# Moving three transposes in a step-scheduled attention and Mamba kernel: the second residual from step 30 to 19, x1 from step 2 to 3

## What is computed

```
q, k, v = wq x + bq, wk x + bk, wv x + bv        # 32, 32 and 256 channels, 4096 positions
x1  = gamma * (v softmax(q^T k)^T) + x            # layer 0: attention over all 4096 positions, and the residual
u   = layernorm over channels(x1) * norm_g + norm_b
z, xBC, dt = in_w u                               # 256, 512 and 4 channels
xBC = silu(causal depthwise conv of 4 taps(xBC) + conv_b)
y   = state space scan over the positions (4 heads of 64, 128 states, decay exp(dt * A)) + Dp * xs
out = out_w (rmsnorm(y * silu(z)) * rms_w)
x   = x1 + out * sigmoid(se2(relu(se1(mean of out over the positions)) ))   # gate per batch and channel
```

## Time and profile before

| | |
|---|---|
| three runs, median | 3153.75 us (3151.14 to 3154.02) |
| the profiled execution | 3150.87 us, its span 3148.7 us |
| TensorE (PE) busy | 2980.0 us, 95% |
| VectorE (DVE) busy | 2032.0 us, 65% |
| ScalarE (ACT) busy | 1930.0 us, 61% |
| GpSimd (POOL) busy | 2009.9 us, 64% |
| mean granted TensorE clock | 0.983 of full speed |

### The profile page before, as it was taken

The page is one execution under the profiler, slowest core; times in us unless marked ns, Lnnn a source line. Parts: engine busy times, 40 slices in busy tenths (PEclk is TensorE's granted clock), DMA queues, the critical chain, the costliest instruction groups (busy, mean ns, idle before and its releaser), DMA issues. The chain is left out here.

```text
span 3148.7 us, 63156 instructions
## 1 busy us (share of the span) xinstructions
PE 2980.0 (95%) x21208; PEld 2322.5 (74%) x21208; DVE 2032.0 (65%) x3417; ACT 1930.0 (61%) x3742; POOL 2009.9 (64%) x3087
## 2 busy tenths in 40 slices
PE   6899999999999999999999999999999999999984
PEld 3767777777777777777777777777777777777762
DVE  5556666666666676676676666676666667666654
ACT  2565666666656566666665666666666666666652
POOL 2446666667756576666676656666676667777753
PEclk9999999999999999999999999999999999999986
DMA  3111111111311121222221222122221111212121
GB/s 123 49 37 46 44 51 58 31 54 49 103 63 65 58 71 58 91 77 74 82 77 38 72 76 72 62 76 69 65 89 36 43 49 55 69 50 69 42 95 67
DMA packets 101970, 200.99 MB, mean 64 GB/s; under 512 B 18480, under 2 KB 41392, under 8 KB 97264
## 3 DMA queue, kind: packets, MB, share of 16 engines
q1 hardware_dynamic: 98192, 195.08, 18.6%
q10 hardware_dynamic: 3456, 1.86, 0.2%
HBM read 131.21 MB, written 64.75 MB: 62 GB/s over the span
## 5 line engine op out<-in xcount | busy, mean ns | idle before, releaser
L723 POOL TENSOR_TENSOR p_lo<-p,p_hi 128x512 f16<-128x512 f32 x1024 | 1221.9, 1201 | 845.6 <-ACT p_hi L886 711.9
L879 ACT ACTIVATE p<-p_et 128x512 f32<-128x512 f32 x1024 | 612.2, 598 | 637.4 <-PE p_et L1138 598.0
L1156 PE MATMUL acc<-v_hi,p_hi 128*128 128x257 f16 x4096 | 954.3, 273 | 4.0 <-DVE work L1464 3.8
L1158 PE MATMUL acc<-v_lo,p_hi 128*128 128x256 f16 x4096 | 951.8, 272 | 0.0
L1420 DVE TENSOR_REDUCE maxes<-p_mx 128x1 f32<-128x1024 f32 x508 | 620.1, 1221 | 489.1 <-PE p_mx L1117 488.7
L886 ACT ACTIVATE p_hi<-p 128x512 f16<-128x512 f32 x1024 | 643.5, 629 | 10.0
L1164 PE MATMUL acc<-v_hi,p_lo 128*128 128x257 f16 x4096 | 622.8, 274 | 15.1 <-POOL p_lo L723 15.1
L1156 PEld LDWEIGHTS acc<-v_hi,p_hi 128*128 128x128 f16 x4096 | 399.3, 97 | 125.0 <-issue 54.8
L1158 PEld LDWEIGHTS acc<-v_lo,p_hi 128*128 128x128 f16 x4096 | 400.6, 98 | 117.8 <-issue 49.9
L1164 PEld LDWEIGHTS acc<-v_hi,p_lo 128*128 128x128 f16 x4096 | 399.9, 98 | 68.0 <-POOL p_lo L723 15.9
L1138 PE MATMUL p_et<-qs,kst 98*128 98x256 f16 x2048 | 393.3, 273 | 11.6 <-ACT p L879 11.1
(11 more groups left out here) (213 smaller groups left out, 4164.2 us busy)
## 6 DMA issues: line engine op xcount, KB each, us to landing
work<-rows_d SPq DMA_DIRECT2D x32, 1024.0 KB, 5.2
xin<-in_x_dram SPq DMA_DIRECT2D x48, 512.0 KB, 4.7
xr<-in_x_dram SPq DMA_DIRECT2D x32, 512.0 KB, 3.8
x_d<-x1c SPq DMA_DIRECT2D x31, 512.0 KB, 2.9
og_d<-og SPq DMA_DIRECT2D x29, 512.0 KB, 2.7
mix_x<-x_d SPq DMA_DIRECT2D x25, 512.0 KB, 4.7
mix_o<-og_d SPq DMA_DIRECT2D x24, 512.0 KB, 5.5
out_dram<-mix_o SPq DMA_DIRECT2D x24, 512.0 KB, 2.8
```

Source lines behind the costliest of these rows:

```text
L723: e.tensor_tensor(p_lo[:, n % RING, :], p32[:, n % P32S, :], p_hi[:, n % RING, :], ALU.subtract).then_inc(lo_pool, 1)
L879: e.activation(p32[:, n % P32S, :], p_et[:, :], ACT.Exp).then_inc(exp_done, 1)
L1156: e.matmul(acc[:, t, 0:C + 1], p_hi[:, r, at:at + P], v_hi[:, 2 * k + kk, 0:C + 1], start=(k == 0 and kk == 0), stop=False)
L1158: e.matmul(acc[:, t, 0:C], p_hi[:, r, at:at + P], v_lo[:, 2 * k + kk, :], start=False, stop=False, skip_group_check=True)
```

## The change

Two constants change, and with them the place of the fill on TensorE, of the copy that empties it on ScalarE, and of the transfer that follows it on SyncE's queue. No instruction is added or removed.

```diff
-K_X1T, K_UT, K_DT, K_DAT, K_CUM, K_YT, K_OUT = 2, 9, 10, 21, 23, 30, 0
+K_X1T, K_UT, K_DT, K_DAT, K_CUM, K_YT, K_OUT = 3, 9, 10, 21, 23, 30, 0
-K_XT = (13, 30)
+K_XT = (13, 19)
```

## The result

| | before | after |
|---|---|---|
| median of five runs | 3153.21 us (3148.49 to 3154.02) | 3136.39 us (3133.51 to 3140.16) |
| the profiled execution, its span | 3150.87, 3148.7 us | 3134.20, 3132.1 us |
| mean granted clock | 0.983 | 0.982 |

The ratio of the runs is 0.9952, with a 95% interval of 0.9938 to 0.9966: faster by 16.8 us by the medians, and by 16.67 us between the two profiled executions. The forecast was 3137.5, in a range of 3123 to 3147.

What follows compares the result with a forecast made beforehand. TensorE, busy 2980.0 of 3148.7 us, was taken as the bound, so gains must come from its waits. Gains of 14.5 and 1.7 summed to 16.2 us, giving 3137.5 us by the median, range 3123 to 3147.

Steps and rivals of the forecast that it cites:

- Part A: Second `xT` moved from step 30 to 19: net 0.56 us less in a regular block, 14.5 us in all.
- the five blocks with a `v`: Blocks 4, 9, 12, 17, 20 at step 30: `v` then waits as `xT` did, winning only 0.13 us each.
- rival 3: The gain of step 30 is given back at step 8 as well: about 3150 us, chance 0.08.
- Rival 5: ScalarE becomes the bound in steps 19 to 21, `xT`'s copy delaying the exponential: 3162 us, chance 0.04.
- Part B: `x1T` moved from step 2 to 3: 0.52 us of wait gone, mostly given back at step 8; 1.7 us gain.
- The shift of GpSimd by the scan: In 19 blocks VectorE's earlier scan holds an earlier Newton step: GpSimd 0.1 us later each, -1.9 us in all.
- Room of 0.1 us before `x1T1`: At step 3, `mt` would end 0.1 us before `x1T1` asks for it: cost nothing, or a few tenths.
- Blocks 10, 18, 26: Blocks with the gate at steps 4 and 7, half a us before GpSimd binds: 0.3 us gain each.
- 8 and 16: Blocks where `mr` behind `st1` waits for VectorE, whose train moves with TensorE: 0.3 us gain each.
- The tail: Blocks 32 on, where `cb0` comes before `x1T` but its waits are for GpSimd: no change.
- Rival 2: The `x1T` move counts too, GpSimd's train being less fixed than it looks: 3123.7 us, chance 0.12.
- Rival 4: Stalls of blocks 9 and 17 lengthen and the slow-clock stretch behind doubles, costing 8 us: 3145 us, chance 0.08.

Runs made afterwards that it cites:

- a_only: Kernel before with only the second `xT` moved from step 30 to 19, `x1T` left at step 2; 3138.1 us, ratio 0.9959.
- ab_sum7: Changed kernel with GpSimd's first output sum moved from step 6 to 7; 3136.64 us, ratio 0.9946 to the kernel before.
- ab_mix14: Changed kernel with VectorE's mix of the previous batch two steps later (T_MIX 12 to 14); 3131.57 us, again 3132.65 us.
- b_only: Kernel before with only `x1T` moved from step 2 to 3, second `xT` left at step 30; 3152.27 us, ratio 1.0003.
- ab_sum7_mix14: Changed kernel with GpSimd's first output sum at step 7 and VectorE's mix at T_MIX 14; 3144.57 us, ratio 0.9964.

## Why the prediction was right, and where it was not

**Part A, 14.5 forecast, 13.7 measured in the tabled steps and 14.5 with the step that the table leaves out.** The step lengths came out to the hundredth: 2.85 and 1.98, net -0.56; in the five blocks with a `v` -0.15 for -0.13. Blocks 2 to 30 make 24 x 0.56 + 5 x 0.15 = 14.2, and the tabled sum has 0.4 less, because only the +0.44 of step 19 of block 31 is inside it. Its step 30 gives 0.77 in the tail, net 0.33 where 0.4 was counted. With it, part A measures 14.5 us. The reasons held too: `a_only` shows no wait at step 8 that grew, so everything behind step 30 does follow TensorE, and rival 3 is out. Rival 5 is out by the row of ScalarE above: the exponential has the room that was worked out.

**Part B, 1.7 forecast; about 1.9 measured without blocks 9 and 17, by other terms.** The cause, that GpSimd's train takes the gain back at step 8, was right (`ab_sum7`). Three of its terms were off:
- *The shift of GpSimd by the scan* had the wrong sign. Steps 2 to 9 of an ordinary block give -0.18, where the forecast had +0.1: GpSimd is 0.18 earlier, not 0.1 later. VectorE's scan and GpSimd's Newton steps after the change, against the earlier trace rows:

```profile
1490.01 1.22 DVE L1561 TENSOR_TENSOR_SCAN lt<-work,ident 128x512 f32<-128x512 f32 x1
```

```profile
1490.19 1.03 POOL L765 TENSOR_SCALAR nw<-nw 128x4 f32<-128x4 f32 x1 [0.16 <-issue]
1491.36 0.20 POOL L767 TENSOR_TENSOR nw<-nw 128x4 f32<-128x4 f32 x1
```

  The scan did hold the Newton step until its own end (1491.23), as the Trainium skill's page "SBUF — State Buffer", section "Who interferes with whom", has it. But it caught L765, one step earlier than before, and not L763: one more step follows behind it, not two. The train loses 0.34 us there and wins the 0.52 by which the scan ends earlier. So an ordinary block gives back 0.34 at step 8 (idle 0.73 for 0.39) where the forecast had 0.6. In blocks 11, 19 and 27 the wait of `st1` is gone behind the new wait for `mt`, and in blocks 14, 22 and 30 it did not grow. Its total is therefore 15.1 and not 23.
- *Room of 0.1 us before `x1T1`* was read off one block and taken for all. It holds in block 15 and in 25 others. In blocks 2, 11, 19 and 27 VectorE's train is later, and the trace of before shows it. Block 11 before, the start of step 2 and `mt`:

```profile
1108.44 0.38 PE L1138 MATMUL p_et<-qs,kst 98*128 98x256 f16 x2
...
1111.70 0.68 DVE L1569 TENSOR_TENSOR mt<-pl,lt 128x512 f32<-128x512 f32 x1
```

  TensorE would ask 2.85 us into the step (2.19 + 0.22 + 0.44), and `mt` ends 3.94 into it, with no idle time before it that could be won: the same sum as for block 15 gives a wait of 1.09 us here and in blocks 2, 19 and 27 (1.10, 1.08 and 1.07). It came as 1.06 in 11, 19 and 27. A small operation of VectorE is held by GpSimd in these blocks. Block 11 after the change, VectorE and TensorE:

```profile
1105.09 1.04 DVE L1477 TENSOR_SCALAR nw<-nw 128x4 int32<-128x4 int32 x1
1106.04 1.21 DVE L1420 TENSOR_REDUCE maxes<-p_mx 128x1 f32<-128x1024 f32 x1
1107.17 0.67 DVE L1569 TENSOR_TENSOR mt<-pl,lt 128x512 f32<-128x512 f32 x1
```

```profile
1107.99 0.63 PE L1171 MATMUL pl<-ident,work 128*128 128x128 f32 x4 [1.06 <-DVE mt L1569]
```

  In block 15 the same L1477 takes 0.49 us. Block 11 has a mix on VectorE at step 0, and with the mix moved away (`ab_mix14`) L1477 is back to 0.50 and the wait is gone. Block 2 has no mix; what makes its VectorE late before the change was not tested. But why its wait is 1.94 and not 1.10 stands in the traces. L1477 and GpSimd's next `low` (L723), before and after:

```profile
254.96 0.17 DVE L1477 TENSOR_SCALAR nw<-nw 128x4 int32<-128x4 int32 x1
255.87 1.16 POOL L723 TENSOR_TENSOR p_lo<-p,p_hi 128x512 f16<-128x512 f32 x1 [1.02 <-ACT p_hi L886]
```

```profile
255.51 1.04 DVE L1477 TENSOR_SCALAR nw<-nw 128x4 int32<-128x4 int32 x1
255.37 1.16 POOL L723 TENSOR_TENSOR p_lo<-p,p_hi 128x512 f16<-128x512 f32 x1
```

  Before, ScalarE's copy of `x1T` stood ahead of `p_hi` in step 2, and GpSimd idled for 1.02 us beside L1477. The change takes that copy away; GpSimd's `low` comes at once, and L1477 lasts 0.87 us longer beside it. Behind this wait the granted clock fell:

```profile
259.00:262.00 3.00, 3.00 (x16) 2.11 (x15) 0.00 (x0) 1.12 (x2) 2.12 (x8) 0.50 0.51 172
```

  All eight traces of kernels with B have this stretch in block 2, none of the six without B has it. The four blocks cost 4.8 us, where the forecast had a gain of 0.5 (block 2) and a loss of 0.3 (the other three). This is the step of part B that failed: *"nothing, or a few tenths"* was 1.06 and 1.94 us of idle time.
- *Blocks 10, 18, 26* gave 0.51 each where 0.3 was taken, and *8 and 16* 0.43 and 0.07 for 0.3 each. Blocks 4, 12 and 20 gave the 0.52 of the forecast.

That the errors of B cancel is luck: its 16 ordinary blocks gave 4.7 us more than forecast, and blocks 2, 11, 19 and 27 gave 5.0 less. That the median agrees with the forecast to 1.1 us is partly luck too: blocks 9 and 17 (+1.5), the rest of the attention and the start (+0.9) and the tail without part A's share (-2.5) were not in the sum, and they too nearly cancel.

**The tail, forecast at nothing.** Of its 3.3 us 0.8 are part A's step 30 of block 31. The other 2.5 are within what the same program shows from one execution to the next, so these traces show nothing against the forecast of no change, and they could not show a change of 1 or 2 us.

**Rival 2** (B counts in full) is out by `b_only`. **Rival 4** (the clock): the stalls of blocks 9 and 17 did grow, from 8.2 us of idle time in sum in both traces of before to 9.5 and 10.1 in the first two of the changed kernel. But both blocks together are 212.6, 211.3 and 211.4 us in three traces against 211.4 and 212.3 before, so the slow stretch did not double. What did come is a new slow stretch in block 2, where the forecast had no stall.

## What to carry to other kernels

When a bank is asked for in the same step in which its neighbour was filled, a move by a single step takes the wait away; look at the order of the fills before looking for a quiet place. A wait taken out of a bound engine counts as far as nothing behind it hangs on a train of another engine that started earlier: find the next wait behind the change and what anchors the engine it names. And the room read in one block is the room of that block: a new wait has to be priced in every kind of block, above all where another engine has a piece of work that comes only sometimes. Here the trace of before already had the four exceptions, at 1.1 us each.

## What the runs showed of the hardware

- A VectorE operation on 128x4 elements (L1477) took 0.17 us while GpSimd was idle (block 2 before) and 0.50 or 1.04 us beside GpSimd's elementwise operations (blocks 15 and 11), and a Newton step of GpSimd 1.20 or 1.03 us instead of 0.20 beside VectorE's scan (block 15 before and after). It goes both ways, so a shift of one train changed the other: the scan's 0.52 us moved GpSimd by 0.18 us in block 15, and GpSimd's `low`, 1.06 us earlier in block 2, made VectorE 0.87 us later.
- The steps of an ordinary block repeat to 0.05 us over five traces of two programs, with few exceptions, while the stretch behind a stall of TensorE doesn't: the granted clock in the same 14 us of one program was 0.86 and 0.57, and the tail 122.9 to 129.5 us. The first and the third profiled execution of the changed kernel differ by 6.75 us, and 6.6 of them are the tail.
- A new stall can cost its own length and, behind it, time at the lower clock: 1.94 us of idle time in block 2 were followed by a granted clock of 0.50 from 259 to 262 us, in all eight traces that have the stall; at step 10 of blocks 11 and 27 of `ab_sum7_mix14`, 0.51 us of idle time by 0.50 for 6 us.
